# A Mamba block and a tree feed-forward on one core: dt's softplus read from PSUM, path sums and first norm at other steps, five instead of six dbu by GpSimd

## What is computed

```python
h = layernorm(x) * (1 + ca) + sa
xp, z = split(h @ W_in); u = silu(causal_conv4(xp) + conv_b)      # 256 channels each
dt_r, B, C = split(u @ W_xp)                                      # 8, 16, 16 columns
delta = softplus(dt_r @ W_dt + dt_bias)
# per channel e and state n (16 of them), over time t:
h_t = exp(delta_t * A[e,n]) * h_{t-1} + delta_t * B_t[n] * u_t    # dA and dbu
y_t = sum_n h_t[n] * C_t[n] + u_t * D
x = x + ga * ((y * silu(z)) @ W_out)
h = layernorm(x) * (1 + cb) + sb
gate = sigmoid((h @ Wq.T) @ routers.T)                            # 255 nodes of a tree
leaf_prob = product of gate or 1 - gate along each of 256 paths
x = x + gb * ((leaf_prob @ leaf_values) @ Wo.T + Wo_b)
```

## Time and profile before

| what | value |
| --- | --- |
| median of three runs | 538.68 us |
| the profiled execution, its time and span | 538.69 us, 536.9 us |
| busy: DVE, POOL, PE, ACT | 454.3, 445.3, 406.6, 374.1 us |
| mean granted clock of TensorE | 0.898 of full |
| first scan to last scan | 29.94 to 512.16 us |

### The profile page before, as it was taken

The page is one execution under the profiler, slowest core; times in us unless marked ns, Lnnn a source line. Parts: engine busy times, 40 slices in busy tenths (PEclk is TensorE's granted clock), DMA queues, the critical chain, the costliest instruction groups (busy, mean ns, idle before and its releaser), DMA issues. The chain is left out here.

```text
span 536.9 us, 6647 instructions
## 1 busy us (share of the span) xinstructions
PE 406.6 (76%) x2104; PEld 278.4 (52%) x2135; DVE 454.3 (85%) x542; ACT 374.1 (70%) x680; POOL 445.3 (83%) x246
## 2 busy tenths in 40 slices
PE   8978834896679757984899747984899758574887
PEld 4436524483548435663567435662557435464554
DVE  6788794998999968998799968997899968998871
ACT  3367774478966888588756898598856886448454
POOL 3468889999899978997799979997889978998800
PEclk8989885899799969998799979999899969785899
DMA  6491062200721073303512063303512063300001
GB/s 169 132 357 75 6 235 89 106 2 21 249 106 62 6 236 117 99 0 125 208 34 89 5 236 117 100 1 131 202 43 81 6 234 118 98 0 2 8 13 39
DMA packets 24867, 53.16 MB, mean 99 GB/s; under 512 B 4601, under 2 KB 13952, under 8 KB 20736
## 3 DMA queue, kind: packets, MB, share of 16 engines
q1 hardware_dynamic: 24832, 52.74, 29.0%
HBM read 50.11 MB, written 2.62 MB: 98 GB/s over the span
## 5 line engine op out<-in xcount | busy, mean ns | idle before, releaser
L561 POOL TENSOR_TENSOR hc<-h,c_rows 128x1024 f32<-128x1024 f32 x126 | 296.6, 2367 | 41.4 <-DVE h L1286 38.0
L1286 DVE TENSOR_TENSOR_SCAN h<-dA,state,dbu 128x512 f32<-128x512 f32 x192 | 234.6, 1270 | 20.1 <-ACT dA L649 19.8
L649 ACT ACTIVATE dA<-delta,a_neg 128x512 f32<-128x512 f32 x256 | 173.1, 684 | 44.5 <-DVE h L1286 43.6
L1065 PE MATMUL yb<-ident,hc 128*128 128x128 f32 x1024 | 155.8, 291 | 22.0 <-POOL hc L561 20.1
L1065 PEld LDWEIGHTS yb<-ident,hc 128*128 128x128 f32 x1024 | 133.3, 152 | 64.7 <-issue 32.4
L548 POOL TENSOR_TENSOR dbu<-du,b_rows 128x1024 f32<-128x1024 f32 x48 | 113.4, 2363 | 4.0 <-DMA b_rows<-bc_dram 4.0
L1299 DVE TENSOR_TENSOR dbu<-du,bb 128x1024 f32<-128x1024 f32 x80 | 96.5, 1206 | 20.5 <-PE bb L1090 10.9
L1286 DVE TENSOR_TENSOR_SCAN h<-dA,dbu 128x512 f32<-128x512 f32 x64 | 74.6, 1210 | 17.8 <-ACT dA L649 17.7
L973 PE MATMUL mf<-f_hT,w_conv 128*128 128x512 f32 x112 | 56.1, 628 | 2.0 <-ACT zu L708 1.4
L996 PE MATMUL mf<-zu,w_xdt 128*128 128x512 f32 x56 | 31.2, 640 | 17.1 <-ACT delta L742 11.5
L824 PE MATMUL mt<-ident,t_xhat 128*128 128x128 f32 x28 | 7.6, 427 | 37.8 <-ACT t_xhat L590 37.8
(11 more groups left out here) (198 smaller groups left out, 544.5 us busy)
## 6 DMA issues: line engine op xcount, KB each, us to landing
c_rows<-bc_dram SPq DMA_DIRECT2D x32, 1024.0 KB, 6.8
b_rows<-bc_dram SPq DMA_DIRECT2D x48, 256.0 KB, 7.3
xs<-in_L_attn_x_dram SPq DMA_DIRECT2D x8, 256.0 KB, 3.8
out_dram<-xs SPq DMA_DIRECT2D x7, 256.0 KB, 5.6
...
w_in<-in_L_attn_W_in_dram SPq DMA_DIRECT2D x1, 256.0 KB, 4.2
```

Source lines behind the costliest of these rows:

```text
L561: nc.gpsimd.tensor_tensor(hc[:, pair % RC, :, :], h[:, pair % RH, :, :], c_rows[:, q, n % NQ, :].unsqueeze(1).broadcast_to([P, HALVES, T]) ...
L649: nc.scalar.activation(dA[ke % RD][:, :], delta[:, ge % 2, half, :], ACT.Exp, scale=a_neg[:, half, n:n + 1]).then_inc(s_dA, 1)
L1065: last = nc.tensor.matmul(bank[:, tile], hc[:, pair % RC, half, tile], ident[:, :], start=False, stop=n == N - 1, is_transpose=True, skip_ ...
L1286: v.tensor_tensor_scan(h[:, pair % RH, half, :], dA[k % RD][:, :], dbu[:, pair % RW, half, :], start, ALU.mult, ALU.add).then_inc(s_scan, 1)
```

## The change

POOL makes dbu of the states 2, 5, 8, 11, 14 instead of 2, 4, 7, 9, 12, 14, and DVE the other eleven. The two halves of dt lie in different banks (half 1 goes to mt, at the same steps) and are not evicted: at step 17 ACT applies softplus with the bias straight from both banks, once for each half, and the separate flags of the halves replace the one of delta. The xd product moves from steps 15, 16 to 18, 19. In the tail the second norm's ACT parts go from steps 15 and 19 to 19 and 24, its turning from 20 to 27, the node products from 28, 30 to 29, 30; the path sums from 22, 24 to 19, 21, the leaf product from 25, 26 to 23, 24, and its adding on DVE from 28 to 24. The first norm's statistics stay at step 19 but are made one group earlier, and the rest of it moves from steps 21, 22, 25 of a group to 2, 3, 6 of the same. In group 0 the tail weights come a few steps earlier.

```diff
-    POOL_N = (2, 4, 7, 9, 12, 14)
+    POOL_N = (2, 5, 8, 11, 14)
...
-    N_STATS, N_RSTD, N_OFF, N_XHAT = 19, 21, 22, 25
-    F_SILU, F_DT, F_SP, F_DU = 10, (13, 15), 17, (25, 26)
+    N_STATS, N_RSTD, N_OFF, N_XHAT = 19, 2, 3, 6
+    F_SILU, F_SP, F_DU = 10, 17, (25, 26)
...
-    T_GATE, T_ADD, T_STATS, T_RSTD, T_OFF, T_XHAT = (4, 5), 12, 12, 15, 16, 19
-    U_FIN = 28
+    T_GATE, T_ADD, T_STATS, T_RSTD, T_OFF, T_XHAT = (4, 5), 12, 12, 19, 20, 24
+    U_FIN = 24
...
-              ("dt", 0): (1, (11, 12)), ("dt", 1): (1, (13, 14)), ("xd", 0): (1, (15, 16)), ("tr", 0): (2, (28,))},
-        "t": {("yt", 0): (-1, (6,)), ("yt", 1): (-1, (8,)), ("out", 0): (-1, (10,)), ("tr", 0): (-1, (20,)),
-              ("lp", 0): (-2, (22,)), ("lp", 1): (-2, (24,)), ("ff", 0): (-2, (25, 26)), ("node", 0): (-1, (28,)),
-              ("node", 1): (-1, (30,))},
+              ("dt", 0): (1, (11, 12)), ("xd", 0): (1, (18, 19)), ("tr", 0): (2, (28,))},
+        "t": {("yt", 0): (-1, (6,)), ("yt", 1): (-1, (8,)), ("out", 0): (-1, (10,)), ("dt", 1): (1, (13, 14)),
+              ("lp", 0): (-2, (19,)), ("lp", 1): (-2, (21,)), ("ff", 0): (-2, (23, 24)), ("tr", 0): (-1, (27,)),
+              ("node", 0): (-1, (29,)), ("node", 1): (-1, (30,))},
...
-    W_TURN, W_COPY, W_MUL, W_TAKE, W_SCALE = (4, 9), (7, 11), 13, 16, 20
+    W_TURN, W_COPY, W_MUL, W_TAKE, W_SCALE = (3, 7), (5, 9), 10, 12, 20
...
+        def wait_delta(eng, g, half):
+
+            if g == 0:
+                eng.wait_ge((s_d0, s_delta)[half], 1)
+            else:
+                wait_read(eng, "ft"[half], "dt", half, g)
...
-                    if front and s in F_DT:
-                        half = F_DT.index(s)
-                        wait_job(act, "f", "dt", half, f)
-                        nc.scalar.activation(delta[:, f % 2, half, :], job("f", "dt", half, f)[1][:, :], ACT.Identity,
-                                             bias=dtb[:, half:half + 1]).then_inc(s_read["f", "act"], 1)
                     if (front or leaf) and s == F_SP:
                         if front:
-
-                            wait_read(act, "f", "dt", 1, f)
-                            both = delta[:, f % 2, :, :]
-                            nc.scalar.activation(both, both, ACT.Softplus).then_inc(s_delta, 1)
+                            for half in range(HALVES):
+                                side = "ft"[half]
+                                wait_job(act, side, "dt", half, f)
+                                nc.scalar.activation(delta[:, f % 2, half, :], job(side, "dt", half, f)[1][:, :],
+                                                     ACT.Softplus, bias=dtb[:, half:half + 1]).then_inc(s_read[side, "act"], 1)
...
-                    if norm and s == N_STATS:
+                    if 2 <= g + 3 < GROUPS and s == N_STATS:
+
                         dve.wait_ge(s_x, 16 * (GROUPS - 2))
-                        stats(m2, f_bn, f_mv, s_fvar)
+                        if g >= 0:
+                            dve.wait_ge(s_fnm, g + 1)
+                        stats(g + 3, f_bn, f_mv, s_fvar)
```

More of the change, by code:

```diff
@@ L564, in _ @@
                         half = F_DU.index(s)
[L565 removed]
+                        wait_delta(pool, f, half)
                         pool.wait_ge(s_silu, f + 1)
```

9 lines of the change are left out of this document (5 added, 4 removed).

## The result

The changed kernel takes 511.74 us (median of four runs, 509.97 to 512.9) where the kernel before takes 538.36 (534.51 to 538.88, four runs beside it). The ratio is 0.9517, with a 95% interval of 0.9465 to 0.957. The forecast was 512.0 in 504 to 530. The profiled execution took 512.9 with a span of 510.9: 25.8 less than the profiled one of before, where the forecast had 27.

A forecast was written before the change was run, and what follows sets the result against it. No engine by share (DVE 85%, POOL 83% busy); DVE's waits for ACT and PE bound it. 41.1 us idle - 7.8 added dbu - 8.2 left + 1.25 + 1.0 = 27.3; 27 off 538.68 gave 512, range 504 to 530.

The forecast's parts named there:

- The sum: Whole kernel: 41.1 us idle less 7.8 added dbu less 8.2 idle left, plus 1.25 and 1.0, gains 27.3 us.
- ACT's pause: Step 17 of a leaf group: from end of scan 16 to end of dA 20 takes 7.15 us, before 8.6.
- DVE's cover: Between scans 16 and 20: 7.0 us of DVE work cuts the wait for dA 20 from 2.73 to 0.15.
- PE's row: Steps 18 to 28: reordered PE work ends the 1.70 and 0.94 waits; scan 28 starts 3.2 us sooner.
- The first norm: Steps 2 and 6: its ACT operations fall where ACT waits for scans; worth nothing, up to 2 us if cover short.
- 1.25 us later, absorbed: Group -1: stats of group 2 delay the first dbu 1.25 us, hidden by scan 13 of group 0 waiting 3.91.
- POOL: Each group: one dbu of 2.363 us less, work about 52 us, 3 to 5 below DVE's new pace; cost nothing.
- Group 0: Group 0: POOL reaches hc of state 10 about 1 us sooner; gain 1.0 us, between 0 and 3.
- That stays: Group 0: path matrices (6.83 us on POOL) and the resulting 6.28 us wait at step 28 would remain.
- PE at half clock: Path sums, six leaf groups: slow clock costs some 3 us each, 530 us; 0.20 shared with the POOL rival.
- The waits that only change their place: Whole kernel: DVE keeps 41.1 us idle and gets the dbu, 548 us; 0.08 shared with the 566 case.
- POOL as the bound: All groups: POOL's 54 us holds them, so only the dbu split gains, about 530 us; 0.20 shared with half clock.

## Why the prediction was right, and where not

**The time.** 512.0 against 511.7, by the mechanism that was forecast. The order, not the split, carries it. That the two times agree within 0.3 us is in part luck: two terms of the sum were off by 3.0 and 1.85 us with opposite signs (below, under The sum), the profiled executions differ by 25.8 and not by 27, and the runs of the changed kernel alone span 2.9 us.

**ACT's pause.** 7.15 us forecast, 7.2 measured. Right, term by term: 1.30 from each table load to what follows it, 0.58 and 0.57 for the softplus. But I put "the xd copy, the two evictions of dt with their waits" in one breath. The runs part them: xd's place with the bank of dt's second half is 14.6 us, the evictions and the softplus nothing or less than nothing. The remark that this work is "worth nothing by itself where ACT isn't late" was right.

**DVE's cover.** Wait for dA 20 forecast 0.15, measured 0.28 in groups 2 and 3, 0.46 in group 4; in groups 5 and 6, without the f stats, forecast 1.4, measured 1.45. The two dbu of the cover were named in the sum but not priced as what they are: take one away and the wait is 1.40.

**PE's row.** Path sums forecast at 5.1 and 10.2, measured at 5.8 and 10.3, the leaf product done at 15.9 in both. bb's wait at step 24 vanished in group 2 as forecast (0.25 is left behind step 28), 0.57 came once in group 5. U_FIN was charged with 0.5; the five waits were 0.43, 0.23, 0.72, 1.44 and 0.42, mean 0.65, so the sum is right, and the one group above 1 is that with the half clock on a path sum.

**The first norm.** "Nothing" is right within the measurement. "1.25 us later, absorbed" is not borne out: with the old steps the first scan starts at 29.02 and the window of group 0 is 72.12 us, in the changed kernel 32.41 and 72.00, so the late start goes through to the end. The times of the two kernels do not differ, and the first scan of the other variants with the new norm lies anywhere from 30.5 to 32.4, so the price of it is small and not settled.

**POOL.** About 52 us a group forecast, 51.1 to 52.1 measured in groups 2 to 6. b rows took 9.0 us from issue to landing (median of 40) instead of 7.3, and POOL's wait for them rose only from 4.0 to 4.3.

**Group 0.** Gain of 1.0 forecast; it ended at 104.41 instead of 105.26, 0.85 less, with the long wait still there at 6.62. The earlier steps of the tail weights are part of that and were not tested alone. What I took as given ("That stays") turned out to be the cheapest 10 us of the kernel.

**The sum.** Idle left in groups 1 to 7 forecast 8.2, measured 11.2, so 3.0 less gain; DVE's work there grew by 4.7 us instead of 6.55, so 1.85 more; group 0 gave 0.85 instead of 1.0. Together 26.0 of span against 27.3. (The bound "505 with no idle left" is 503 by the terms of the sum; nothing hangs on it.) Group by group 0.6, 0.9, 0.9, 0.9, 2.1, 2.1, 0.7 against 0.99, 1.08, 1.02, 1.93, 3.59, 2.21, 0.37. The excess lies in groups 4 and 5: 0.72 and 1.44 at U_FIN, and 0.57 for bb in the group with the half clock.

**The rivals.** PE at half clock: of the six leaf groups, it fell on path sums in group 5, where it cost 1 to 2 us, and on the first one of group 7 (1.93 a pair), where DVE waits no more than 0.37 in the whole window; 18 was the price in all. In the kernel before the first path sum ran at 1.9 to 2.1 a pair in five of the six. By the Trainium skill, "TensorE: Matmul & The Clock Gate", section "HAM oscillation — how this bites in real kernels", the slow clock should go with the wait inside the loop; at this place the trace agrees, 0.89 over steps 17 to 24 instead of 0.73. It came back behind another wait, of 3.65 us at step 28, and the mean clock of the execution is 0.903 against 0.898. The waits that only change their place: refuted, 11.2 us instead of 41.1. POOL as the bound: refuted by the kernel before with five states, which is slower. The Trainium skill, "Perfetto Trace Analysis", section "Identifying the Most-Contended Engine", has the engine of highest occupancy optimized first. Taken as giving that engine less work, the trace does not agree while it has waits: DVE at 85% was given 6.5 us more and the kernel gained 5%, because what fell were DVE's waits. Less work on it counts once the waits are gone: then one dbu less on DVE, in the right place, went with 0.1 to 0.9 us a group.

What each part of the change is worth, from the kernels that lack it: the place of xd with the bank of dt's second half 14.6 us, the leaf's and tail's row 8.4, the split 3.4, the form of the softplus -1.8 (within the error), the first norm -0.4 (likewise). Together 24.2 of 26.6; the parts overlap, so no exact sum is to be expected.
